# Attention shifts of two head pairs in one step: from 64-row products ahead of each pair's scores to 32-row products at the head of the step

## The reference

```python
x = x + attention(_layernorm(x), Wq, Wk, Wv, Wp, bp)   # 16 heads of 64
x = x + ffn(_layernorm(x), ...)                        # ternary weights, 128 -> 512 -> 128, gelu

q = einsum('bnd,hde->bhne', query, Wq) / sqrt(64)
k = einsum('bmd,hde->bhme', query, Wk)
logits = einsum('bhne,bhme->bhnm', q, k)
attn = softmax(logits, axis=-1)
out = einsum('bhnm,bhme->bnhe', attn, v)
```

## Time and profile before

| what | before |
|---|---|
| median of 3 runs | 1001.01 us |
| lowest and highest run | 1000.87, 1002.82 us |
| span of the profiled execution | 998.7 us |
| the median less that span | 2.3 us |
| granted TensorE clock | 1.000 of full |
| TensorE, VectorE, ScalarE, GpSimd busy | 980.8, 880.0, 729.6, 837.1 us |

### The profile page before, as it was taken

One profiled execution on the slowest core, in us unless ns is written; L12 is line 12 of the kernel. 1 busy time (PEld: TensorE's weight loads), 2 busy tenths in 40 slices (PEclk: granted clock), 3 DMA queues, 4 the chain that ended last, 5 costly groups with the idle time before them and its releaser, 6 DMA issues.

```text
span 998.7 us, 39391 instructions
## 1 busy us (share of the span) xinstructions
PE 980.8 (98%) x16052; PEld 782.2 (78%) x16052; DVE 880.0 (88%) x1779; ACT 729.6 (73%) x1151; POOL 837.1 (84%) x861
## 2 busy tenths in 40 slices
PE   7899999999999999999999999999999999999998
PEld 6577777778777787887887777888878777788886
DVE  7888988988889888898889988889889988788998
ACT  5687677777767777777777777777777776879995
POOL 6789888989887888888899888888888889866765
PEclk9999999999999999999999999999999999999999
DMA  6112332222331232233222233324222233354343
GB/s 141 38 32 51 53 66 45 43 49 52 74 53 27 51 73 53 52 53 71 55 48 41 48 73 51 53 53 71 46 41 47 52 52 53 69 86 75 77 86 65
DMA packets 203682, 57.82 MB, mean 58 GB/s; under 512 B 185072, under 2 KB 203248, under 8 KB 203504
## 3 DMA queue, kind: packets, MB, share of 16 engines
q1 hardware_dynamic: 201424, 54.79, 29.8%
q10 hardware_dynamic: 2080, 0.52, 0.2%
HBM read 7.21 MB, written 4.19 MB: 11 GB/s over the span
## 4 chain that ended last, share of the span: by engine, by line
PE 95%; DVE 2%; ACT 1%; issue 1%; POOL 1%; DVEq 0%; POOLq 0%; ACTq 0%
PE S L675 11%; PE PV L700 8%; PE M L635 7%; PE PV L702 6%; PE PV L701 6%; PE QK L622 5%; PE QK L623 5%; PE QK L624 5%; PE misc L675 5%; PE S L667 5%; PE S L864 3%; PE M L753 2%; PE M L718 2%; PE M L754 2%; PE M L755 2%; PE misc L667 2%
## 5 line engine op out<-in xcount | busy, mean ns | idle before, releaser
L1210 POOL TENSOR_TENSOR pl<-p 128x1024 f16<-128x1024 f32 x253 | 476.9, 1896 | 39.3 <-ACT p L1000 39.1
L1410 DVE TENSOR_REDUCE negmax<-M 128x4 f32<-128x1024 f32 x252 | 306.8, 1217 | 22.4 <-PE M L635 16.4
L1008 ACT ACTIVATE QKh<-QK 128x512 f16<-128x512 f32 x251 | 149.5, 596 | 155.5 <-PE QK L624 155.3
L1000 ACT ACTIVATE p<-S,s_exp 128x1024 f32<-128x1024 f32 x173 | 192.4, 1112 | 71.8 <-PE S L675 71.2
L700 PEld LDWEIGHTS PV<-V,p 128*128 128x128 bf16 x2048 | 186.8, 98 | 46.4 <-issue 34.5
L700 PE MATMUL PV<-V,p 128*128 128x65 f16 x2048 | 214.9, 194 | 4.0 <-DVE O L1424 2.9
L701 PE MATMUL PV<-V,p 128*128 128x64 f16 x2048 | 213.4, 193 | 0.0
L702 PE MATMUL PV<-V,pl 128*128 128x65 f16 x2048 | 212.6, 194 | 0.0
L1430 DVE TENSOR_TENSOR QKl<-QK,QKh 128x512 f16<-128x512 f32 x251 | 172.4, 687 | 42.2 <-ACT QKh L1008 41.1
L701 PEld LDWEIGHTS PV<-V,p 128*128 128x128 bf16 x2048 | 189.1, 97 | 4.7
L702 PEld LDWEIGHTS PV<-V,pl 128*128 128x128 f16 x2048 | 188.7, 97 | 0.0
(11 more groups left out here) (236 smaller groups left out, 2501.6 us busy)
## 6 DMA issues: line engine op xcount, KB each, us to landing
result<-X SPq DMA_DIRECT2D x15, 256.0 KB, 2.6
X<-in_L_attn_query SPq DMA_DIRECT2D x7, 512.0 KB, 4.8
OT<-O SPq DMA_TRANSPOSE x64, 4.6
shift<-negmax SPq DMA_TRANSPOSE x63, 2.3
O<-in_L_attn_Wk ACTq DMA_DIRECT2D x2, 256.0 KB, 4.3
O<-in_L_attn_Wq SPq DMA_DIRECT2D x2, 256.0 KB, 4.5
O<-in_L_attn_Wv SPq DMA_DIRECT2D x1, 512.0 KB, 3.9
w<-in_L_ffn_w SPq DMA_DIRECT2D x2, 256.0 KB, 5.6
```

What stands on the lines that cost most here:

```text
L1000: e.activation(p32[r][:, :, :, :].rearrange("p i m n -> p (i m n)"), score_bank(p)[:, :], ACT.Exp, scale=s_exp[:, :]).then_inc(s_ex, 1)
L1210: e.tensor_tensor(pl[r][:, :, :, :].rearrange("p i m n -> p (i m n)"), p32[r][:, :, :, :].rearrange("p i m n -> p (i m n)"), p_high(r).rea ...
L1410: e.tensor_reduce(dst[:, :, NB * jj:NB * jj + NB], max_bank(p)[:, :].rearrange("p (i t m) -> p i t m", i=2, t=NB), AX.X, ALU.max, negate=T ...
```

## The change

In double steps the four 64-row shift products of each pair are taken out of `scores`. A new function, `shifts_of_two`, makes the shifts of both pairs at the head of the double step, ahead of the wait for M and of the first maximum. The even pair's maxima are laid in the first 32 rows of each head's half and the odd pair's in the other 32 (`shift_row`, `quarter_rows`), so a product has 32 rows. Four products in a row (even pair, both heads; odd pair, both heads) use four different row groups and write the four banks of S and misc. The number of shift products per double step stays at eight, each of 256 columns. Both waits for an exponential stand now ahead of the first shift. In single steps the order of the products is as before, and only the wait for `QKl` moves behind the shifts. `sel8` and `sel` (made once on GpSimd), the rounding on ScalarE and the columns that the reductions write follow the new layout.

```diff
--- before.py
+++ after.py
@@ -147,6 +147,11 @@
 def low_on_pool_before(p):
 
     return p - sum(d < p for d in LOW_ON_DVE)
+
+
+def shift_row(jj, t):
+
+    return GP * (jj % 2) + NB * (jj // 2) + t
 
 
 def shift_group(t):
@@ -432,6 +437,15 @@
 
             return slice(i * E, (i + 1) * E)
 
+        def quarter_rows(i, odd):
+
+            return slice(i * E + odd * E // 2, i * E + (odd + 1) * E // 2)
+
+        def score_tile(p, i, t):
+
+            o = score_bank(p)[:, i * 512:(i + 1) * 512]
+            return o.rearrange("p (m n) -> p m n", m=NB)[:, :, t * P:(t + 1) * P]
+
         def p_high(r):
 
             words = p32[r][:, :, :, :].rearrange("p i m n -> p (i m n)").bitcast(BF16)
@@ -637,24 +651,15 @@
                         if t == NB - 1:
                             op.then_inc(s_ms, 1)
 
-            def scores(p):
+            def shifts_of_one(p):
                 g, jj = divmod(p, GP)
-                h, lo = QKh[p % QK_RING], QKl[p % QK_RING]
                 if p == 0:
                     e.wait_ge(s_sh16, 1)
                     e.wait_ge(s_mx, GP)
+                    e.wait_ge(s_sel, 1)
                 elif jj == 0:
                     e.wait_ge(shift_in, 16 * g)
-                if p == 0:
-                    e.wait_ge(s_sel, 1)
-                e.wait_ge(s_qklo, p + 1)
-                bank = score_bank(p)
-                if p == TWO_0 + 1:
-                    e.wait_ge(s_x1, TWO_0 // HP - 2)
-                    e.wait_ge(s_vlo, v_no[TWO_0 // HP, 3])
-                elif TWO_0 + 1 < p < TWO_1:
-                    e.wait_ge(s_ex, p - 1)
-                elif p == PAIRED:
+                if p == PAIRED:
                     e.wait_ge(s_mx, NP)
                 elif p > PAIRED:
                     e.wait_ge(s_ex, p - 1)
@@ -663,10 +668,30 @@
                 for t in range(NB):
                     for i in range(2):
                         rows = head_rows(i)
-                        o = bank[:, i * 512:(i + 1) * 512].rearrange("p (m n) -> p m n", m=NB)[:, :, t * P:(t + 1) * P]
-                        e.matmul(o, sel[rows, NB * jj + t, :],
+                        e.matmul(score_tile(p, i, t), sel[rows, shift_row(jj, t), :],
                                  shift[g % 2][rows, :].unsqueeze(1).to_broadcast([E, NB, P]),
                                  start=t == 0, stop=False, skip_group_check=True)
+
+            def shifts_of_two(p):
+                g, jj = divmod(p, GP)
+                if jj == 0:
+                    e.wait_ge(shift_in, 16 * g)
+                e.wait_ge(s_ex, p)
+                if p == TWO_0:
+                    e.wait_ge(s_x1, TWO_0 // HP - 2)
+                    e.wait_ge(s_vlo, v_no[TWO_0 // HP, 3])
+                for t in range(NB):
+                    for odd in range(2):
+                        for i in range(2):
+                            rows = quarter_rows(i, odd)
+                            e.matmul(score_tile(p + odd, i, t), sel[rows, shift_row(jj + odd, t), :],
+                                     shift[g % 2][rows, :].unsqueeze(1).to_broadcast([E // 2, NB, P]),
+                                     start=t == 0, stop=False, skip_group_check=True)
+
+            def scores(p):
+                h, lo = QKh[p % QK_RING], QKl[p % QK_RING]
+                e.wait_ge(s_qklo, p + 1)
+                bank = score_bank(p)
                 for m in range(NB):
                     tok = slice(m * P, (m + 1) * P)
                     for n, (k, q) in enumerate(((h, h), (h, lo), (lo, h))):
@@ -756,6 +781,7 @@
                 op.then_inc(s_yp0 if t == 0 else s_yp, 1)
 
             def two_steps(t):
+                shifts_of_two(t)
                 if t > TWO_0:
                     e.wait_ge(*two_free(t - 2))
                 max_scores(t + MAX_LEAD)
@@ -808,6 +834,7 @@
             def step(t):
                 b, j = divmod(t, HP)
                 if 0 <= t < NP:
+                    shifts_of_one(t)
                     scores(t)
                 if t == TWO_1:
                     e.wait_ge(*two_free(t - 2))
@@ -987,7 +1014,8 @@
                     e.wait_ge(shift_in, 16 * (g - 2))
                 elif g == 1:
                     e.wait_ge(s_const, 3)
-                e.activation(negmax16[g % 2][:, :, 0:2 * GP], negmax[g % 2][:, :, :], ACT.Copy,
+                e.activation(negmax16[g % 2][:, :, :].rearrange("p i (o c) -> p (i o) c", o=2)[:, :, 0:GP],
+                             negmax[g % 2][:, :, :].rearrange("p i (o c) -> p (i o) c", o=2), ACT.Copy,
                              scale=1.0 / SHIFT_UP).then_inc(s_sh16, 1)
 
             def exps(p):
@@ -1305,7 +1333,9 @@
                             pattern=[[-1, P]], channel_multiplier=1).then_inc(s_ident, 1)
 
             e.wait_ge(s_ident, 2)
-            e.tensor_tensor(sel8[:, :], ident[:, 0:2 * GP], ident[:, E:E + 2 * GP], ALU.add).then_inc(s_ident, 1)
+            quarters = ident[:, :].rearrange("p (i o c) -> p i o c", i=2, o=2)
+            e.tensor_tensor(sel8[:, :].rearrange("p (o c) -> p o c", o=2), quarters[:, 0, :, 0:GP], quarters[:, 1, :, 0:GP],
+                            ALU.add).then_inc(s_ident, 1)
             e.wait_ge(s_ident, 3)
             e.tensor_scalar(sel[:, :, :], sel8[:, :].unsqueeze(2).to_broadcast([P, 2 * GP, P]), SHIFT_UP, None,
                             ALU.mult).then_inc(s_sel, 1)
@@ -1406,8 +1436,10 @@
                 e.wait_ge(s_ms, 2 * p + 2)
                 if jj == 0 and g >= 2:
                     e.wait_ge(s_sh16, g - 1)
-                dst = negmax[g % 2] if g else first_max
-                e.tensor_reduce(dst[:, :, NB * jj:NB * jj + NB], max_bank(p)[:, :].rearrange("p (i t m) -> p i t m", i=2, t=NB),
+                dst, row = negmax[g % 2] if g else first_max, shift_row(jj, 0)
+                if not g:
+                    row += jj % 2 * (E // 2 - GP)
+                e.tensor_reduce(dst[:, :, row:row + NB], max_bank(p)[:, :].rearrange("p (i t m) -> p i t m", i=2, t=NB),
                                 AX.X, ALU.max, negate=True).then_inc(s_mx, 1)
 
             def sums_inverse(p):
```

## The result

| what | before | after |
|---|---|---|
| median of the timed runs | 1001.34 us (4 runs) | 1009.33 us (4 runs, 1009.31 to 1009.45) |
| span of the profiled execution | 998.7 us | 1007.6 us |

The change makes the kernel slower: the ratio is 1.0078, with a 95% interval of 1.0066 to 1.0089. The spans differ by 8.9 us. The page of the changed kernel has the same number of TensorE products as the earlier trace rows and nearly the same busy time, over a longer span.

What follows compares the result with a forecast made beforehand. The loop of first maximum, reduction, QKl, second reduction, then values or projection was taken as the bound. 40 steps ending with values x 0.13 plus 40 with projection x 0.08 gave 8.4 us more: 1009.4 us, range 1002 to 1015.5.

Steps and rivals of the forecast that it cites:

- Two slots of four, 0.23 us: Ahead of the first maximum: two added slots of four 32-row products, 0.11 us each, 0.23 after a change of height.
- Rivals 3 and 4: A slot of four exceeds 0.11 us: 1015.3 us, chance 0.11; the four don't run side by side: 1027, chance 0.04.
- The change from 32 to 64 rows, 0.09 us: Between the new shifts and the first maximum: an added change of tile height, taken to cost 0.09 us.
- Rival 1: The 32-to-64 change of height is free: +1.2 us, 1002.2 us, no difference; chance 0.14.
- First maximum at L + 0.53: First maximum starts 0.53 us after the start of the last query/key product before the double step; before, 0.20 or 0.30.
- The second maximum at L + 2.27: TensorE reaches the second maximum at 2.07 but waits for the first reduction until 2.27: 0.20 us stall per double step.
- To the second reduction 0.67: In VectorE's chain after the first maximum: 0.67 us from QKl's start to the second reduction's start.
- the sum of 3.56 us: From first maximum to values or projection: 0.46, 1.14, 0.67, 1.23 and 0.06 us, through both reductions and QKl.
- TensorE would be there at 4.00: At values or projection: TensorE alone arrives at 4.00, then waits 0.09 us for VectorE's second reduction, until 4.09.
- No cost behind that point, none for the moved waits: After values or projection, order and lengths stand; the exponential and turned-shift waits moved ahead of the shifts cost nothing.
- No slack for a later start: The loop from first maximum through both reductions to values or projection cannot absorb a later start.
- Rival 2: VectorE does not hold TensorE, whose own work decides: 13.6 us less, 987.4 us, faster; chance 0.06.

Runs made afterwards that it cites:

- the third slot: The changed kernel with a third slot of four 32-row products per double step, the first slot made twice: 1018.73 us, ratio 1.0173.

## Why the prediction was right, and where it was not

**The time** was forecast at 1009.4 us and measured at 1009.33, slower by 0.78%. The working had 8.4 us more; the spans differ by 8.9 us and the medians by 8.0. Most steps of the working held. Two readings of the chain between the maxima were wrong, and in the sum they cancelled, which was luck.

- *Two slots of four, 0.23 us:* 0.12 and then 0.11 us, shown by the timeline and by the third slot. Rivals 3 and 4 fall. The estimate by the Trainium skill's 3.07x ("TensorE: Matmul & The Clock Gate", Measured speedup vs the span model), 1.30 slots for four, does not describe this case at 256 columns.
- *The change from 32 to 64 rows, 0.09 us:* right; 502.02 follows the slot of 501.82 by 0.20. Rival 1 falls. The Trainium skill's "TensorEngine Tiling (Array Packing)", Tiling Modes, has a drain of the array at such a change. The trace agrees that this one costs, as much as the other two, but the next product starts at 502.02, before the last record ends at 502.09.
- *First maximum at L + 0.53:* right, in both kinds of step.
- *The second maximum at L + 2.27, a stall of 0.20 us in each step, 16 us in all:* wrong. It starts at 2.37, and the stall is 0.29, 23 us in all. I took 0.06 us for the semaphore from the wait for V. The second maximum stands behind a separate wait instruction and pays 0.146. The V-step of before showed it: its first reduction ends at 500.17 and its second maximum starts at 500.32, 0.15 us later. The prediction did not measure that gap, and it expected no wait of this kind before the change.
- *"To the second reduction 0.67":* wrong in what it is. I read it as VectorE's QKl. With the waits swapped it is 0.60; the other 0.07 is the wait for the second maximum's products, which are late by the separate wait. The rows of before had the sign: the second reduction starts 0.44 us after the second maximum in the V-step and 0.45 in the P-step, while from QKl it is 0.67 and 0.83. So the wait that was missing in the one step stood in the other, and the sum of 3.56 us was right. Had the 0.83 of the P-step been taken, the same sum would have given 4.25.
- *"TensorE would be there at 4.00", so that VectorE's reduction holds the values:* wrong by the same 0.09. Both arrive at 4.09, as the shortened second reduction shows (1.1 us less, where the working would have given 7).
- *No cost behind that point, none for the moved waits:* right. The first 32-row product starts at L + 0.205 in both kinds of step, as the first maximum did in the V-step. The steps are longer by 0.14 and 0.08 us, just as values and projection are later, and that makes up the 8.9 us between the spans.
- *"No slack for a later start":* not so in the V-step of before, though the sum doesn't use it. There the first reduction waits for a layer norm's statistics on VectorE and starts 0.69 us after the first maximum instead of 0.46 (498.29, 498.98). So 0.22 us of the maximum's delay of 0.33 cost nothing. The timeline of VectorE, before:

```profile
498.30 0.48 DVE L1387 BATCH_NORM_STATS2 st<-X 128x6 f32<-128x128 f32 x2
498.81 0.25 DVE L1390 BATCH_NORM_AGGREGATE mv<-st 128x2 f32<-128x6 f32 x2
```

- *Rival 2, TensorE's own work decides:* false for the changed kernel. The shortened first reduction shows about what it would have given, 987 us; the rival's working had 987.4.

In sum: the first maximum came 0.33 us later in V-steps (0.20 to 0.53) and 0.23 in P-steps (0.30 to 0.53). Between the two maxima 0.44 us of work went, but the time there fell only by 0.19 (2.02 to 1.83) and 0.15 (1.98 to 1.83), because the reduction and its waits now fill it. The differences, 0.14 and 0.08 us, are the loss of each kind of step.

## What to carry to other kernels

Where a single buffer ties two engines in a loop, look for the instruction that starts the loop. Work moved ahead of it is paid except as far as the loop stood there for something else, and work removed behind it is worth only what the other engine's part of the loop doesn't cover. Measure from start to start for both engines before counting slots. Compare the gap after each release with the other gaps of this kind. If one is larger (0.146 beside 0.057 us) and stays the same from step to step, the instruction does wait for that release, and the difference is a cost that can be removed by itself.

## What the runs showed of the hardware

- Four products of 32 rows and 256 columns, in four row groups and four banks, start 2 to 4 ns apart and take one slot, 0.11 us (the third slot of four, 0.109). Two products of 64 rows, or one of 128, also take 0.109 us in the changed kernel.
- After each change of tile height the next product starts 0.20 us after the last product's start. It costs 0.09 us between 128 and 64, from 128 to 32 and between 32 and 64 rows alike. The first slot of 32-row or 64-row products behind such a change takes 0.12 us instead of 0.11.
- An instruction that waits for two semaphores in this program has one of the waits as an instruction of its own. If that one is released last, the product starts 0.146 us after the releasing instruction's end instead of 0.057, and the waits view says "issue" in place of the releaser. In `max_scores` the wait written last was the separate one. Swapping the two calls gave 5.9 us in the changed kernel and 1.9 us in the one before.
